# Four gated layers on one core: context attention with its sums per quad and their inverses on ScalarE, and more unread products on TensorE

## What is computed

```
for i in 0..3:
    x = x + tanh(g_xattn[i]) * xattn_i(layernorm(x), context)
    x = x + tanh(g_ffn[i])   * ffn_i(layernorm(x))
```

```
a = softmax(einsum('bhsd,bhtd->bhst', q, k) * D ** -0.5)      # H, D = 16, 32; t = 77 in a2
o = einsum('bhst,bhtd->bhsd', a, v)                            # heads joined
x_out = x + o @ li1_w + li1_b
h = gelu(_ln(x_out) @ li2_w + li2_b);  return x_out + h @ li3_w + li3_b
```

## Time and profile before

| | us |
|---|---|
| three runs | 1722.56, 1711.97, 1721.43 |
| median | 1721.43 |
| the profiled execution | 1725.82 |
| its span, first to last instruction | 1724.0 |
| its mean granted TensorE clock | 0.934 |

### The profile page before, as it was taken

The page is one execution under the profiler, slowest core; times in us unless marked ns, Lnnn a source line. Parts: engine busy times, 40 slices in busy tenths (PEclk is TensorE's granted clock), DMA queues, the critical chain, the costliest instruction groups (busy, mean ns, idle before and its releaser), DMA issues.

```text
span 1724.0 us, 21952 instructions
## 1 busy us (share of the span) xinstructions
PE 1498.8 (87%) x8790; PEld 670.3 (39%) x8790; DVE 869.3 (50%) x1674; ACT 744.3 (43%) x1313; POOL 148.7 (9%) x209
## 2 busy tenths in 40 slices
PE   5849999998999989988579999888999889888296
PEld 2223323342444436623133333423444357333294
DVE  4475776453566452334645874524664542455212
ACT  2554556423454225343544556243454253342043
POOL 0000111100012000000000112000021000020331
PEclk9968999998999889998789999999999999989598
DMA  5000000000000100000000000000000000030341
GB/s 202 1 1 0 1 2 1 0 1 1 0 1 1 50 1 0 1 1 2 1 1 1 1 1 1 0 1 1 1 2 18 33 1 1 1 85 1 91 134 62
DMA packets 18105, 30.27 MB, mean 18 GB/s; under 512 B 4640, under 2 KB 12640, under 8 KB 17104
## 3 DMA queue, kind: packets, MB, share of 16 engines
q1 hardware_dynamic: 16752, 26.23, 4.8%
q0 software_dynamic: 1248, 2.59, 0.4%
HBM read 23.62 MB, written 5.19 MB: 17 GB/s over the span
## 4 chain that ended last, share of the span: by engine, by line
PE 79%; DVE 10%; ACT 7%; issue 2%; DMA 1%; POOL 1%; SPq 0%; POOLq 0%; DVEq 0%; ACTq 0%
PE ps L837 7%; PE ps L944 5%; PE ps L711 4%; PE ps L883 4%; PE ps L1423 3%; PE ps L1409 3%; PE ps L750 3%; PE ps L651 3%; PE ps L1077 3%; PE ps L1085 2%; PE ps L997 2%; PE ps L896 2%; PE ps L975 2%; PE ps L688 2%; PE ps L684 2%
## 5 line engine op out<-in xcount | busy, mean ns | idle before, releaser
L2115 DVE TENSOR_REDUCE peak<-ps 128x1 f32<-128x512 f32 x256 | 163.2, 682 | 90.5 <-PE ps L837 90.5
L1726 ACT ACTIVATE big<-ps 128x512 f32<-128x512 f32 x256 | 138.5, 596 | 112.9 <-PE ps L875 112.2
L837 PE MATMUL ps<-pp,qT 32*128 32x512 f32 x512 | 147.7, 661 | 1.4 <-ACT pp L1849 1.4
L866 PE MATMUL ps<-qT,pp 32*128 32x512 f32 x512 | 148.1, 654 | 0.0
L1749 ACT ACTIVATE big<-ps 128x512 f32<-128x512 f32 (+3 forms) x256 | 101.1, 436 | 101.5 <-PE ps L975 100.5
L2160 DVE TENSOR_REDUCE crest<-ps 128x2 f32<-128x512 f32 (+3 forms) x128 | 105.4, 824 | 56.3 <-PE ps L950 56.0
L975 PE MATMUL ps<-qT,pp 32*128 32x128 f32 (+3 forms) x512 | 123.1, 479 | 0.0
L1665 ACT ACTIVATE big<-ps 77x1024 f32<-77x1024 f32 x96 | 93.1, 1016 | 67.7 <-PE ps L711 67.7
L2056 DVE TENSOR_REDUCE small<-ps 128x8 f32<-128x616 f32 x96 | 76.8, 800 | 80.7 <-PE ps L684 46.4
L944 PE MATMUL ps<-pp,qT 32*128 32x384 f32 (+3 forms) x512 | 105.3, 480 | 3.5 <-DVE crest L2160 1.5
L1645 ACT ACTIVATE sq<-ps 128x512 f32<-128x512 f32 x48 | 28.7, 597 | 171.7 <-PE ps L651 171.7
(11 more groups left out here) (492 smaller groups left out, 2646.7 us busy)
## 6 DMA issues: line engine op xcount, KB each, us to landing
big<-in_w SPq DMA_DIRECT2D x23, 256.0 KB, 3.3
pt<-in_l2w SPq DMA_DIRECT2D x2, 2048.0 KB, 7.7
w_l<-in_l SPq DMA_DIRECT2D x1, 3086.0 KB, 17.7
pp<-in_w SPq DMA_DIRECT2D x1, 2048.0 KB, 9.5
big<-by_expert SPq DMA_DIRECT2D x23, 66.0 KB, 2.0
by_expert<-cst SPq DMA_DIRECT2D x1, 1472.0 KB, 16.5
cst<-in_const SPq DMA_DIRECT2D x1, 1427.5 KB, 6.5
w_l<-in_l SPq DMA_DIRECT2D x1, 1218.0 KB, 8.7
```

The costliest lines, as they stand in the source:

```text
L837: pe.matmul(rbank(x), qT[at, u, k, 128 * i:128 * i + 128], keyT(u, k)[at, :], start=True, stop=True, tile_position=(32 * c, 0)).then_inc(* ...
L866: pe.matmul(a1_bank(y), keyT(u, k)[at, 128 * j:128 * j + 128], qT[at, u, k, :], start=True, stop=False, tile_position=(32 * c, 0))
L1726: A(prob(m)[:, TURN_OF[g], :], a1_bank(tplace(m, g)), ACT.Exp).then_inc(*SCALAR.did("a1", "exp", m, g))
L2115: v.tensor_reduce(peak[:, p // 4 % 2, i, c:c + 1], rbank(ring(p, c)), AX.X, ALU.max)\
```

## The change

Two things are done.

a2's sums: `sums` now multiplies by ones, a quad at a time and without accumulation, so that bank 1 holds each head's sum on all of its 32 rows. ScalarE takes Ln and Exp(-x) of it (`inverted`) and VectorE multiplies the values in bank 0 by that (`over`) straight into `qT`. The evictions, the reciprocals and the spreading products are gone. The output projection is done inside `cross` (`li1`), slot 0's before the last sums and values of slot 1.

Unread products: `norm` on TensorE issues `behind` of them after its second mean product (and `late` more after the first slot's result; in four norms with context projections it waits first for VectorE to have read bank 2), and bursts are put at other waits.

```diff
@@ cross, all engines
+        def inverses(u, k):
+            return (rs if k % 4 < 2 else sq)[:, k % 2, :]
@@ TensorE
-            def norm(tag, src, ready, dim=128):
+            def norm(tag, src, ready, behind, late=0):
...
                     pe.matmul(aux(u), K["mean"], sq[:, u, :], start=True, stop=True).then_inc(*TENSOR.did(tag, "v", u))
+                if tag in ("l0x", "l2x", "l3x", "l1c"):
+                    pe.wait_ge(*VECTOR["a2" if tag == "l1c" else tag, "kv", 0])
+                unread(scb(0), behind)
+                if late:
+                    pe.wait_ge(*VECTOR[tag, "n", 0])
+                    unread(scb(0), late)
@@ sums
-                    if u and k == 0:
-                        pe.wait_ge(*SCALAR[tag, "den", 0])
+                    if u or k:
+                        pe.wait_ge(*SCALAR[tag, "log", u if k else 0, (k - 1) % 4])
                     for c in range(4):
-                        mm = pe.matmul(PSB[1][32 * c:32 * c + 32, :],
-                                       K["col8"][0:KC, 128 * k + 32 * c:128 * k + 32 * c + 32], cprob(u, k)[:, c, :],
-                                       start=k == 0, stop=k == 3, tile_position=(0, 32 * c), skip_group_check=True)
+                        mm = pe.matmul(PSB[1][32 * c:32 * c + 32, :], K["ones"][0:KC, 0:32], cprob(u, k)[:, c, :],
+                                       start=True, stop=True, tile_position=(0, 32 * c), skip_group_check=True)
@@ values
-                        pe.wait_ge(*SCALAR[tag, "o", u if k else 0, (k - 1) % 4])
+                        pe.wait_ge(*VECTOR[tag, "O", u if k else 0, (k - 1) % 4])
@@ cross, end
+                def li1(u):
+                    if u == 0:
+                        pe.wait_ge(*SCALAR[tag, "exp", 1, 5])
+                    for c in range(4):
+                        pe.wait_ge(*VECTOR[tag, "O", u, c])
+                        mm = pe.matmul(PSB[4 + u], W["l1"]["a2_li1"][:, 128 * c:128 * c + 128], qT[:, u, c, :], start=c == 0,
+                                       stop=c == 3)
+                    mm.then_inc(*TENSOR.did("a2 li1", u))
...
+                else:
+                    li1(0)
                 sums(1, 3)
                 values(1, 3)
                 if dh == 8:
                     shares(1)
-                    return
-                for u in U:
-                    pe.wait_ge(*VECTOR[tag, "inv", u])
-                    for k in range(4):
...
-                        mm.then_inc(*TENSOR.did(tag, "spread", u, k))
+                else:
+                    li1(1)
@@ attend, before turned(0)
+                pe.wait_ge(*SCALAR["a1 made", 20])
+                unread(PSB[0], 7)
@@ start of the turn
+                unread(lin(0), 4)
@@ feed-forward of layer 0, before the transposes of q1
+                unread(scb(3), 6)
+                pe.wait_ge(*VECTOR["l0f a", "offset"])
+                unread(scb(3), 6)
+                pe.wait_ge(*VECTOR["l0f inverse", 50, 0])
+                unread(scb(3), 6)
                 for u in U:
+                    if u:
+                        unread(scb(3), 6)
                     pe.wait_ge(*(VECTOR if u else SCALAR)["l0f q1", u])
@@ before the transposes of q2
+                for moment in (SCALAR["l0f gelu", 0], SCALAR["l0f gelu", 1], VECTOR["l0f inverse", 60, 1]):
+                    pe.wait_ge(*moment)
+                    unread(aux(0), 7)
+                pe.wait_ge(*SCALAR["l0f rounded", 0])
+                unread(aux(0), 6)
@@ ScalarE, cross with dh == 32
+                def inverted(u, k):
+                    act.wait_ge(*TENSOR[tag, "den", u, k])
+                    if u:
+                        act.wait_ge(*VECTOR[tag, "O", 0, k])
+                    A(inverses(u, k), PSB[1], ACT.Ln).then_inc(*SCALAR.did(tag, "log", u, k))
+                    act.wait_ge(*SCALAR.last())
+                    A(inverses(u, k), inverses(u, k), ACT.Exp, scale=-1.0).then_inc(*SCALAR.did(tag, "inv", u, k))
...
+                        for a in range(8):
+                            exp(u, a)
+                            if a >= 3 and a % 2:
+                                inverted(u, a // 2 - 1)
+                        inverted(u, 3)
+                        if u == 0:
+                            shifted(1)
@@ VectorE, cross with dh == 32
-                def inverse(u):
-                    v.wait_ge(*SCALAR[tag, "den", u])
-                    v.reciprocal(rs[:, u, :], sq[:, u, :]).then_inc(*VECTOR.did(tag, "inv", u))
+                def over(u, k):
+                    v.wait_ge(*TENSOR[tag, "AV", u, k])
+                    v.wait_ge(*SCALAR[tag, "inv", u, k])
+                    v.tensor_tensor(qT[:, u, k, :], PSB[0], inverses(u, k), ALU.mult).then_inc(*VECTOR.did(tag, "O", u, k))
...
                         maxima(u, a)
+                        if dh == 32 and u and a % 2 and a > 1:
+                            over(0, a // 2 - 1)
                     cut_off(u)
...
+                over(0, 3)
+                for k in range(4):
+                    over(1, k)
```

More of the change, by code:

```diff
@@ L646, in _, with unread @@
             ident = K["ident"]
-            def norm(tag, src, ready, dim=128):
+            def unread(bank, n):
+                for _ in range(n):
+                    pe.matmul(bank, identb[:], w1q[:], start=True, stop=True)
+            def norm(tag, src, ready, behind, late=0):
                 for u in U:
@@ L1260, in _ @@
                 cross("a2", 32)
-                reduce4("a2 li1", w["a2_li1"], lambda u: qT[:, u, :, :],
-                        lambda u: [SCALAR["a2", "o", 1, 3], VECTOR["a2", "O", u, 3]])
-                norm("a2n3", lambda u: x2[:, u, :], lambda u: VECTOR["a2 x2", u])
+                norm("a2n3", lambda u: x2[:, u, :], lambda u: VECTOR["a2 x2", u], 5)
                 mlp("a2m", w["a2_li2"], w["a2_li3"])
-                norm("l1f", lambda u: xs[:, u, :], lambda u: VECTOR["l1 res", u])
+                norm("l1f", lambda u: xs[:, u, :], lambda u: VECTOR["l1 res", u], 3)
                 w = W["l1f"]
@@ L1356, in _ @@
                         gates(n // 14, False)
-                norm("l1g", lambda u: x2[:, u, :], lambda u: VECTOR["l1f x2", u])
+                norm("l1g", lambda u: x2[:, u, :], lambda u: VECTOR["l1f x2", u], 0)
                 w = W["l2"]
                 pe.wait_ge(loaded["l2"], 16)
+                unread(scb(0), 6)
                 context_kv("l2x", w["Wk"], w["Wv"], cs, 8)
-                norm("l2x", lambda u: xs[:, u, :], lambda u: VECTOR["l1f res", u])
+                norm("l2x", lambda u: xs[:, u, :], lambda u: VECTOR["l1f res", u], 4)
                 linear("l2x q", w["Wq"], lambda u: xn[:, u, :], lambda u: [VECTOR["l2x", "n", u]])
@@ L1370, in _ @@
                     mm.then_inc(*TENSOR.did("l2x S", u))
+                unread(lin(0), 6)
                 for u in U:
@@ L1381, in _ @@
                 pe.transpose(scb(3)[0:E2, 0:128], w["be2"], ident).then_inc(*TENSOR.did("l2f b2"))
-                norm("l2f", lambda u: xs[:, u, :], lambda u: VECTOR["l2x res", u])
+                norm("l2f", lambda u: xs[:, u, :], lambda u: VECTOR["l2x res", u], 4)
                 for u in U:
@@ L1668, in out @@
                 def out(u, k):
[L1669 removed]
                     if dh == 8:
+                        act.wait_ge(*TENSOR[tag, "AV", u, k])
                         if k % 2:
@@ L1687, in cross @@
                 shifted(0)
+                if dh == 32:
+                    for u in U:
+                        for a in range(8):
[5 more added lines that the diff above has]
+                            shifted(1)
+                    return
                 for a in range(8):
@@ L1699, in cross @@
                         out(1, (a - 5) // 2)
-                if dh == 8:
-                    share(0)
-                    out(1, 3)
-                    inverse(0)
-                    share(1)
-                    inverse(1)
-                    return
-                out(1, 2)
+                share(0)
                 out(1, 3)
+                inverse(0)
+                share(1)
+                inverse(1)
             def attend():
@@ L2098, in cross @@
                     return
-                for u in U:
-                    inverse(u)
-                for u in U:
-                    for k in range(4):
-                        v.wait_ge(*TENSOR[tag, "spread", u, k])
-                        v.wait_ge(*SCALAR[tag, "o", u, k])
-                        v.tensor_tensor(qT[:, u, k, :], qT[:, u, k, :], PSB[2 + (4 * u + k) % 6], ALU.mult)\
-                            .then_inc(*VECTOR.did(tag, "O", u, k))
+                over(0, 3)
+                for k in range(4):
+                    over(1, k)
             def attend(residual_of):
```

32 lines of the change are left out of this document (8 added, 24 removed).

## The result

The changed kernel takes 1673.01 us (median of four, 1666.57 to 1681.3) against 1721.99 of the kernel before, run beside it: a ratio of 0.9736, 95% interval 0.9691 to 0.9782. The forecast was 1679, range 1659 to 1705. Six later runs gave a median of 1680.62 (1666.4 to 1681.88), ratio 0.9758 (0.9719 to 0.9798); over all ten it is 1679.4. Ten executions of this one kernel spread over 15 us; the experiments (e11, e6) find one cause of such differences, a stretch at the lower clock that comes in some executions and not in others. How much of the spread it makes is not measured, since only profiled executions can be taken apart. The profiled execution took 1676.56 us, span 1674.8 against 1724.0, mean granted clock 0.970 against 0.934.

What follows compares the result with a forecast made beforehand. TensorE was taken to bound the kernel (79% of the chain), partly at the lower clock. The a2 change, 26 us, and the unread products, 16, made 42 off: 1679 us against the median 1721.43, range 1659 to 1705.

Steps and rivals of the forecast that it cites:

- Part A: Layer 1's context attention (a2), sums divided by quad without spreading products: 27.7 us worked out, 26 taken, bounds 15.9 and 29.
- B1: Rival, chance 0.15: slot 1 of a2 falls to the lower clock again, a2's change gives 16 us, time 1689.
- Part B: Unread products at norms, feed-forward, layer 2 and elsewhere hold the clock up: 27.4 us worked out, 16 taken, bounds nothing and 27.4.
- norms with the projection: Five norms of the two turns in low stretches, and the projections behind one, at full clock: 10.1 us gained.
- layer 2: From its transposes to the router at full clock: 3.7 us gained, 2.9 in turn 2, 6.6 together.
- start of the self-attention: Layer 1, from `turned(0)` to the first sums, at full clock: 4.0 us gained, 1.7 in turn 2, 5.7 together.
- feed-forward: Its tail of some 60 small products at full clock: 2.4 us per turn less 0.4, so 4 gained.
- turn's change: Unread products at the turn's ends hold the clock up: 1 us gained.
- The burst of 13: Feed-forward, 7 and 6 unread products behind the second inverse: they do not fit their wait and cost 0.4 us per turn.
- C: Rival, chance 0.18: the unread products lift nothing that counts and give 0, time 1695; with B1 1705.
- D: Rival, chance 0.05: the unread products run at the lower clock and overrun their waits, 12 us per turn, 24 in all.
- C2: Rival, chance 0.10: everything works and turn 1's low stretch at 593 to 603 stays away by luck, time 1661.

Runs made afterwards that it cites:

- e11: The changed kernel run again as it is, for a second profile and six more timed runs: median 1680.62 us, ratio 0.9758.
- e6: The changed kernel with five more unread products per turn among layer 1's experts: 1670.03 us, ratio 0.9731.
- e10: The changed kernel with slot 0's half of `li1` put behind the last values of slot 1 in place of ahead of the last sums: 1678.68 us.
- e1: The changed kernel without any of the new unread products, only the new a2 attention: 1693.31 us, ratio 0.9848.
- e2: The kernel before with all 133 unread products per turn and the old a2: 1698.56 us, ratio 0.9886.
- e8: The changed kernel without the four unread products at a turn's start and the feed-forward's last six (seven stay behind the second inverse): 1667.56 us, ratio 0.9722.
- e5: The changed kernel with twice as many unread products behind each norm (6 to 12 in place of 3 to 6): 1675.38 us.
- e3: The changed kernel without the 51 unread products per turn in the feed-forward: 1683.62 us, ratio 0.9798.
- e9: The changed kernel with the edits of e6 and e8 and with unread products behind the loop: 1659.49 us (six runs), ratio 0.9655.

## Why the prediction was right

**The sum** was worked as 27.7 + 27.4, taken as 26 + 16 = 42; measured by pieces 28.4 + 21.2 = 49.6; the untouched pieces and the later start cancelled by chance (+2.7, -2.9, +0.65). The median of four lies 6 us below the forecast, that of all ten on it, and this is partly luck: the two profiled executions differ by 49.2 us, but that of the kernel before was 4.4 slower than its median and that of the changed one 2.8 faster than its ten, which brings 49.2 down to the 42 forecast. The choice of three fifths for B was too low: four fifths of the worked value came.

**Part A, slot 1.** 21.2 us were worked out, 20.78 measured, in both turns. Of the 1.8 us of waits, 1.1 came: the scores of the first two quads take 3.64 us (384.47 to 388.11) where two quads' scores take 2.5 later, because of the bank of the first exponential. The profile shows only 0.25 of it as idle time, as the products come two at a time there. The other 0.7, waits for the division in three quads, did not come, and both halves of `li1` take 7.17 where 6.97 was said. Slot 0's end costs 0.60 where 0.5 was said, and values(0, 3) waits 0.30 for VectorE. Slot 0's quad stayed at 5.50 us. One reason was wrong and did no harm to the sum: that `li1` moved ahead fills a wait for the last exponential. The exponential is done at 396.33, 0.1 us into `li1`; the move is worth 1.05 us per turn (e10), not the 3.5 that it lasts.

**B1** (slot 1 falls to the lower clock) is refuted: the new slot has no low microsecond in any of the 22 turns of eleven profiles, two of them with no new unread product at all (e1). What the forecast named as the reason, the 1.50 us wait in front of the fall, stands again in e2, with 1.49 us in turn 1, though in turn 2 the first such wait passes without a fall. The clock's part of A's gain is 3.5 to 5.2 and 2.0 to 3.7 us; half of a stretch of 13.4 and 10.1 us, 6.7 and 5.0, had been said. The old slot was less bound by TensorE than supposed.

**Part B by place.** Forecast and measured, both turns together: norms with the projection 10.1, 5.9; layer 2 6.6, 8.5; start of the self-attention 5.7, 5.5; feed-forward 4, 3.9; turn's change 1, and it lost 2.6 (2.0 in e11). Norms and layer 2 share a norm, so their sum, 16.7 and 14.4, is the fair comparison. The term that had the wrong sign is the turn's change: its four products were taken as hidden, but in turn 2 they run at the lower clock, 1.87 us, in front of data that is ready, and turn 1 loses 0.55 (e8). The burst of 13 was given 0.4 us of overrun and has 0.47 (e8).

**C** (B gives nothing) is refuted by e2 alone: 20.4 us without A. **D** (overrun) has the right mechanism in one place, the turn's start; its price at the norms is refuted by e5: ten products take 2.16 us there, as long as the rival's five at the lower clock, and cost 1.0 us per turn, not 6: a part of each overrun is swallowed where another engine sets the next piece. **C2's** luck is the stretch among the experts: not an event of turn 1 alone, but one that came in 13 of 22 turns, worth 6 us or more in eight of them. The forecast's main case had no term for it, and a median of four could have come out several microseconds lower or higher.

**On the two rules of the Trainium skill** ("TensorE: Matmul & The Clock Gate"). Section "HAM oscillation — how this bites in real kernels" ties a fall to TensorE standing idle for a while. In e11 the clock falls at 569.5 with no idle time over 0.72 us since 561.1; the runs speak against the rule as the only cause. Section "Part 4: PE-mode transpose" says that transposes don't count as activity. In e3 the clock stays low through 7.40 us of transposes and small products, in e8 seven products ahead of the same transposes keep it at full; but e3 also has 10.47 us of idle time ahead of them, so it doesn't separate the two. That was not tried apart and stays open.

**Open** too: what decides whether the clock falls among the experts. The two bands and the grid describe it over 22 turns; the reason is not known. Whether the five products prevent it rests on one turn that stood in a band and on the timed runs; which of the five would do it was not tried.

## What to carry to other kernels

A low clock costs only where TensorE sets the pace: cut the span at the same events in two profiles and price each piece, and don't count low microseconds (20 of them cost 0.3 us in one place, 7 cost 2.0 in the next). Put an unread burst ahead of such a piece, so short that it ends before its input is there, and never where the engine is at the lower level with work ready. Where two runs of one kernel differ by more than what is measured, look for the piece that differs before pooling the medians; here six runs of e9 lay within 4.9 us where six of the changed kernel spread over 15.5, and the last comparison was sharp.

## What the runs showed of the hardware

- The granted clock falls in the middle of nearly dense work: in the changed kernel at 1295.5 and in e11 at 569.5, both times in the same wait of 0.72 us, the longest in the nine microseconds before it, among eight-row and eight-column products. TensorE is busy for 2.02 of the 2.50 us before 1295.5 (first window; the second is the stretch). With five products of 128 rows and 512 columns among them it stayed up in four turns of e6 and e9.

```profile
1293.00:1295.50 2.50, 2.02 (x10) 0.96 (x9) 1.55 (x7) 0.00 (x0) 0.00 (x0) 1.00 0.00 0
1295.50:1312.60 17.10, 16.49 (x36) 5.75 (x36) 6.21 (x23) 1.78 (x4) 0.00 (x0) 0.50 0.00 0
```

- Two executions of one program differ by whole stretches of the lower clock, while most pieces without one agree to 0.02 us over all the kernels here.
- Products of eight columns feel the clock too: 32 of them took 6.64 us in a low stretch and 3.71 at full clock, a factor of 1.8. The column scores of e2 went from 1.10 to 2.01, also 1.8.
